# Transposing the row maxima of two sets at once, and loading them in four transfers a half

## The reference, cut to what matters

```python
scores = jnp.einsum('bhqd,bhkd->bhqk', q, k) / jnp.sqrt(jnp.asarray(HEAD_DIM, q.dtype))
weights = jax.nn.softmax(scores, axis=-1)
ctx = jnp.einsum('bhqk,bhkd->bhqd', weights, v)
```

## Time and profile before

| | us |
|---|---|
| median of three runs (575.12 to 579.55) | 578.35 |
| the profiled execution | 579.48 |
| its span in the trace | 577.7 |

### The profile page before, as it was taken

One profiled execution on the slowest core, in us unless ns is written; L12 is line 12 of the kernel. 1 busy time (PEld: TensorE's weight loads), 2 busy tenths in 40 slices (PEclk: granted clock), 3 DMA queues, 4 the chain that ended last, 5 costly groups with the idle time before them and its releaser, 6 DMA issues.

```text
span 577.7 us, 12491 instructions
## 1 busy us (share of the span) xinstructions
PE 486.3 (84%) x3970; PEld 404.6 (70%) x3970; DVE 349.5 (60%) x1226; ACT 315.4 (55%) x675; POOL 201.9 (35%) x429
## 2 busy tenths in 40 slices
PE   1447999899998899975799999999999897599980
PEld 1336777668776588964677877777777687599970
DVE  7886687688775146756587778678678433112203
ACT  2214776677766535553476666575566654245640
POOL 7140002221222222444211112442543657765650
PEclk9998999899999999995799999999999998789995
DMA  6314333242321992004454324234320110222107
GB/s 179 94 37 131 118 101 98 78 129 89 97 66 67 412 364 74 2 1 125 133 184 141 96 63 140 87 101 125 107 72 17 52 46 18 80 83 72 43 19 218
DMA packets 52267, 60.06 MB, mean 104 GB/s; under 512 B 7633, under 2 KB 43354, under 8 KB 50928
## 3 DMA queue, kind: packets, MB, share of 16 engines
q1 hardware_dynamic: 47248, 52.99, 29.3%
q0 software_dynamic: 2272, 4.24, 2.3%
q10 hardware_dynamic: 2688, 2.10, 1.1%
HBM read 30.01 MB, written 29.23 MB: 103 GB/s over the span
## 4 chain that ended last, share of the span: by engine, by line
PE 49%; issue 4%; DVE 4%; ACT 4%; DMA 4%; POOL 3%; SPq 1%; POOLq 0%; ACTq 0%; DVEq 0%
PE ps L1483 6%; PE ps L1536 5%; PE ps L1724 5%; PE ps L1714 5%; PE ps L1519 5%; PE ps L1539 5%; PE ps L1448 2%; PE ps L1450 2%; PE ps L1449 2%; ACT probs L901 2%; PE ps L1677 1%; PE ps L1548 1%; DMA k_blocks<-y_dram 1%; PE ps L1775 1%; DMA k_dram<-qk_parts 1%
## 5 line engine op out<-in xcount | busy, mean ns | idle before, releaser
L901 ACT ACTIVATE probs<-ps 128x512 f32<-128x512 f32 x256 | 146.7, 598 | 81.0 <-PE ps L1539 77.3
L1519 PE MATMUL ps<-k_blocks,q_stacks 128*128 128x256 f32 x512 | 119.4, 317 | 15.9 <-DVE row_max L1135 8.4
L1143 DVE CUSTOM_DVE_ANT_0 ps<-ps,mask_q 128x256 f32<-128x256 f32 x256 | 102.7, 452 | 37.5 <-PE ps L1519 36.6
L1539 PE MATMUL ps<-q_stacks,k_blocks 128*128 128x256 f32 x512 | 106.4, 292 | 1.0 <-DMA q_stacks<-maxT 0.8
L1135 DVE TENSOR_REDUCE row_max<-ps 128x2 f32<-128x512 f32 x128 | 84.3, 687 | 34.5 <-PE ps L1519 33.3
L1539 PEld LDWEIGHTS ps<-q_stacks,k_blocks 128*128 128x128 f32 x512 | 87.5, 190 | 21.0 <-issue 10.5
L1519 PEld LDWEIGHTS ps<-k_blocks,q_stacks 128*128 128x128 f32 x512 | 81.3, 197 | 22.6 <-DVE row_max L1135 12.2
L1483 PE MATMUL ps<-probs,v_aug 128*32 128x256 f32 x1024 | 69.4, 389 | 5.5 <-ACT probs L901 4.5
L763 POOL TENSOR_SCALAR max_split<-row_max 128x16 fp32r<-128x16 f32 x32 | 6.5, 204 | 182.6 <-DVE row_max L1135 79.6
L1536 PE MATMUL ps<-mask_k,neg_mask_eye 128*128 128x512 f32 x128 | 54.3, 424 | 0.4 <-DMA q_stacks<-maxT 0.4
L708 POOL DMA_INDIRECT y_dram<-x_ring x39 | 41.0, 1051 | 25.6 <-ACT x_ring L1000 19.9
(11 more groups left out here) (211 smaller groups left out, 836.7 us busy)
## 6 DMA issues: line engine op xcount, KB each, us to landing
slots_dram<-x_ring SPq DMA_DIRECT2D x1, 10400.0 KB, 29.5
q_stacks<-q_dram SPq DMA_DIRECT2D x32, 256.0 KB
q_dram<-qk_parts SPq DMA_DIRECT2D x16, 384.0 KB, 3.7
k_dram<-qk_parts SPq DMA_DIRECT2D x16, 384.0 KB, 4.0
k_blocks<-k_dram SPq DMA_DIRECT2D x128, 48.0 KB
x_ring<-slots_dram SPq DMA_DIRECT2D x39, 65.0 KB, 2.0
ctx_in<-ctx SPq DMA_DIRECT2D x16, 128.0 KB, 2.2
mask_in<-mask_Bx1xSxS_ik SPq DMA_DIRECT2D x8, 256.0 KB, 3.0
```

The source lines that it names most:

```text
L901: eng.activation(probs[:, n // HPS % 2, n % HPS, :, :].rearrange("p k q -> p (k q)"), ps[:, head_bank(BANKS_T, n)[0], :], ACT.Exp).then_in ...
L1143: last = eng.tensor_tensor_reduce(out=scored, in0=scored, in1=mask_q[1 - r][:, i, :], scale=1.0, scalar=-3.0e38, op0=ALU.add, op1=ALU.max, ...
L1519: mm = eng.matmul(ps[:, bank, i * S:(i + 1) * S], q_stack[r][:, st, i * P:(i + 1) * P], k_blocks[r][:, st, j, :], start=True, stop=True)
L1539: mm = eng.matmul(ps[:, bank, k * S:(k + 1) * S], k_blocks[r][:, st, j, k * P:(k + 1) * P], q_stack[r][:, st, :], start=(l == 0), stop=(l ...
```

## The change

`max_split` is laid out with the two sets of a half beside each other, so a tile's 16 columns (2 sets x 2 parts x 4 heads) are transposed at once. There are two transposes a half instead of four, each 16x128 out. ScalarE's copy is 16x256 instead of 8x512. In `maxT` the sets now lie on different partitions, so the loads into `q_stacks` are made for each set and part: four transfers a half, of four rows of 256 elements, instead of two of four rows of 512. The counts that are awaited go from 2 to 4 transfers.

```diff
-        maxT = sb("maxT", [2 * HPS, 2, 2, S])
+        maxT = sb("maxT", [2 * 2 * HPS, 2, S])
...
             eng.wait_ge(a.mT_sb, b * 2 + half + 1)
-            for part in range(2):
-                eng.dma_start(q_stack[r][part:part + (HPS - 1) * HR + 1:HR, 2 * half:2 * half + 2, :].bitcast(F32),
-                              maxT[part * HPS:(part + 1) * HPS, half, :, :]).then_inc(a.m_in[half], DMA)
+            for st in range(2):
+                for part in range(2):
+                    rows = slice((st * 2 + part) * HPS, (st * 2 + part + 1) * HPS)
+                    eng.dma_start(q_stack[r][part:part + (HPS - 1) * HR + 1:HR, 2 * half + st, :].bitcast(F32),
+                                  maxT[rows, half, :]).then_inc(a.m_in[half], DMA)
...
                 if after(b, 0):
-                    eng.wait_ge(a.m_in[half], b * 2 * DMA)
+                    eng.wait_ge(a.m_in[half], b * 4 * DMA)
                 elif l == 1:
-                    eng.wait_ge(att[0].m_in[half], NB * 2 * DMA)
+                    eng.wait_ge(att[0].m_in[half], NB * 4 * DMA)
                 bank = (BANK_M, BANK_O[0])[half]
-                eng.activation(maxT[:, half, :, :].rearrange("p s q -> p (s q)"), ps[0:2 * HPS, bank, :],
-                               ACT.Copy).then_inc(a.mT_sb, 1)
+                eng.activation(maxT[:, half, :], ps[0:2 * 2 * HPS, bank, 0:S], ACT.Copy).then_inc(a.mT_sb, 1)
...
                 if n % 8 == 0:
-                    eng.wait_ge(a.m_in[n // 8], (b + 1) * 2 * DMA)
+                    eng.wait_ge(a.m_in[n // 8], (b + 1) * 4 * DMA)
...
                 eng.wait_ge(a.m_split, b * 2 + half + 1)
-                for st in range(2):
-                    for i in range(NT):
-                        mm = eng.transpose(ps[0:2 * HPS, bank, st * S + i * P:st * S + (i + 1) * P],
-                                           max_split[:, i, half, st, :, :].bitcast(F32).rearrange("p m j -> p (m j)"),
-                                           ident[:, :])
+                for i in range(NT):
+                    mm = eng.transpose(ps[0:2 * 2 * HPS, bank, i * P:(i + 1) * P],
+                                       max_split[:, i, half, :, :, :].bitcast(F32).rearrange("p s m j -> p (s m j)"),
+                                       ident[:, :])
                 mm.then_inc(a.mT_ps, 1)
```

## The result

The changed kernel takes 584.03 us (median of 5 runs, 582.40 to 585.62) where the kernel before takes 578.81 (median of 5, 575.12 to 579.55). The ratio on record is 1.0119, its 95% interval 1.0090 to 1.0149; the quotient of these two medians is 1.0090, at the interval's lower end. A second series on another occasion gave 1.0111 (1.0072 to 1.0150), with medians 6.3 us apart. So the change costs 5.2 us by the first pair of medians and 6.4 to 6.9 by the ratios. Its profiled execution took 584.33 us with a span of 582.5 us, against 579.48 and 577.7 before.

The account below looks back on a forecast made before the run. The maxima transfers' landing bounds the first stage, TensorE's work the second. First stage +4.0, second -1.6 and clock +2.4 us give +4.8 on 579.48, so 584.3 us profiled and 583 us median, range 577 to 588.

Parts of the forecast that it names:

- Two more issues, 1.1 us: On SyncE's queue, each half's two added maxima transfers were to take 1.1 us more to issue.
- Both bounds: Limits for the two added issues on SyncE: 0.6 us at the k loads' pitch, 2.4 us with a landing added.
- The landing opens every batch of the first stage, 1.3 us behind the last issue: First stage: TensorE starts each batch when the last maxima transfer lands, about 1.3 us after its issue ends.
- faster rival: First-stage openings: the landing does not release them, added issues are hidden, transposes save 5.8 us, total 572.5 us; chance 0.06.
- Five waits for `max_split` swallow 2.7 us: At five first-stage openings, TensorE's waits for GpSimd's split, 2.7 us in all, were to absorb part of the delay.
- Transposes, 0.18 us a group: On TensorE, two transposes fewer save 0.18 us per group: 9 groups in the first stage, 15 in the second.
- The copy, 385 ns: ScalarE's copy was to fall from 578 to 385 ns, with 0.1 us left on the path where it releases SyncE.
- Both stages without the clock, +2.4 us: Both attention stages before clock effects: first stage +4.0 us, second stage -1.6 us, together +2.4 us.
- The second stage keeps its room: Second stage: the landing's 1.38 us to spare ahead of TensorE's opening was to shrink to 0.3 us and hold.
- Two more stretches at the lower clock, +2.4 us: TensorE behind the openings of batch 1 and the second stage: longer waits lower the clock, 1.2 us each.
- rival with the lower clock at nearly every opening: Steady batches' waits of 1.1 to 1.5 us also lower TensorE's clock, five more stretches, near 589 us; chance 0.17.
- The base: Starting time for the sum: the profiled execution's 579.48 us, 1.1 us above the runs' median of 578.35.

Follow-up runs that it names:

- e8: Changed kernel with half 0's rows of 256 each moved in two transfers of 4x128, eight in half 0 and four in half 1; 629.0 us, 1.0886 of before.
- e7: Kernel before with the second of half 0's two maxima transfers issued by ScalarE instead of SyncE; 576.7 us, 0.9996 of before.
- e10: The change in half 0 alone, half 1 as in the kernel before; 584.5 us, 1.0120 of before.
- e4: Changed kernel with only the first set's two transfers per half, the second set's maxima not loaded or subtracted; 574.7 us, 0.9960 of before.
- e1: Kernel before with four maxima transfers of 4x256 in both halves, old transposes and copy; 584.2 us, 1.0118 of before.
- e2: Kernel before with four maxima transfers in half 0 alone, two in half 1, old transposes; 585.2 us, 1.0128 of before.
- e6: Changed kernel with the second set's two transfers of half 0 issued by ScalarE, the first set's by SyncE; 578.0 us, 1.0008 of before.
- e3: Kernel before with four maxima transfers in half 1 alone, two in half 0, old transposes; 577.2 us, 1.0007 of before.
- e9: The change in half 1 alone, half 0 as in the kernel before; 574.0 us, 0.9939 of before.
- e11: Changed kernel with matmuls that nobody reads put ahead of TensorE's waits; 578.9 us, 1.0031 of before.

## Why the prediction was right, and where it was not

583 us was predicted, in a range of 577 to 588, and 584.0 came. The change costs 5.2 us by the first series' medians and 6.4 to 6.9 by the ratios, and the sum said 4.8. The mechanism was right: SyncE's two added issues delay the landing that opens the batches. That the number came so close is in part luck, since errors of several terms cancel. Its steps:

- **Two more issues, 1.1 us.** Right: 2.15 to 2.19 us for four. Both bounds are excluded (e8: 0.54 us each at eight).
- **The landing opens every batch of the first stage, 1.3 us behind the last issue.** Right for the kernel before (the table above). What the step missed is that a smaller transfer lands sooner: 1.15 to 1.26 us for 4x256, and 1.07 to 1.18 for the 4x128 of e8. The openings came later by 1.08 - 0.15 = 0.93 us and not by 1.1, some 1.3 us less over eight. The faster rival falls with the same table; at the opening that e7 lets one compare, the landing was last by 0.16 us.
- **Five waits for `max_split` swallow 2.7 us.** Right: 2.7 us before, none after.
- **Transposes, 0.18 us a group.** The size was 0.22. The count was wrong in the second stage: 15 groups were counted, and the 7 of half 0 give nothing. There the next matmul of the scores starts 0.35 us behind four transposes (376.40 to 376.75) and 0.34 behind two (382.74 to 383.08); ahead of its weight load the changed kernel's row names VectorE's `row_max`. The period fell by 0.23 where 0.36 was predicted; e10 shows the zero of half 0 by itself. For the first stage the step had this distinction and was right.
- **The copy, 385 ns.** 361 ns. The 0.1 us that it was to give SyncE at an opening did not come at the steady ones: the gap between the k loads and the group is 0.12 us before and 0.13 after (162.76 + 1.68 to 164.57).
- **Both stages without the clock, +2.4 us.** Span x clock rose by 1.8 to 2.0. Within it e4 and the changed kernel put the two issues at +5.0 to 5.4 us (e1 and e2 against before: +4.0 and +4.8); e4 against before, and the changed kernel against e1, put transposes and copy at -2.2 to -3.6. Each is a quarter to a half smaller than in the sum (7.2 and 4.8), with some 2 us of uncertainty in each difference, and the errors cancel. That is luck. The steady period was to be 18.4 and is 18.22.
- **The second stage keeps its room.** Right, and with more than the 0.3 us predicted. SyncE's group and TensorE's opening in a steady batch (answers to the earlier trace rows):

```profile
383.84 2.15 SPq L489 DMA_DIRECT2D q_stacks<-maxT  x4
```

```profile
387.50 0.49 PE L1520 MATMUL ps<-k_blocks,q_stacks 128*128 128x256 f32 x2
387.83 0.40 PE L1537 MATMUL ps<-mask_k,neg_mask_eye 128*128 128x512 f32 x1
```

  With the 1.18 us of the first stage the group would open TensorE at 385.99 + 1.18 = 387.17, and TensorE comes at 387.83, 0.66 us later, without a wait. e8 confirms it from the other side: 2.16 us more in the group, and waits of 1.26 to 1.69.
- **Two more stretches at the lower clock, +2.4 us.** This is the term that was mis-sized most: it is +4 to 5 us in the mean of the runs, with some 2 us of uncertainty. It named batch 1 and the second stage's opening. The second came (0.77 and 0.86 above, and likewise in both profiles of the changed kernel and those of e1, e2 and e10). It is not the maxima's wait alone that brings it: e6 has it behind the opening too (0.59) without such a wait, and e4 has a stretch of 0.57 just ahead of its opening (293 to 297 us) and 1.00 behind it. e3, e7 and e9 run at 1.00 there. Behind batch 1 the clock was 1.00 in the changed kernel's first profile and 0.66 in its second, which had a low stretch behind batch 2 as well and none behind batch 3. The step reasoned from which single wait had been followed by a low clock in one execution; between executions of one kernel it is not the same wait. The rival with the lower clock at nearly every opening did not come at waits of 0.7 to 1.4 us; it came at 2.8 to 3.3 us (e8), behind most openings.
- **The base.** The profiled execution of the kernel before had a clock of 0.951 and 28.3 us in the clock's share, where its 63 later runs have 24.0 to 25.3 in the mean. The two profiles at the head therefore show the same clock, 0.951, and hide the clock's part of the loss. That base was 1 to 2 us too high and the increment 2 us too small, which is why the predicted time came out closer than the working deserved.

The Trainium skill ("TensorE: Matmul & The Clock Gate", section on oscillation in real kernels) describes a kernel whose clock falls in every tile because the waits for transfers are long against the work between them, and says to arrange the work so that TensorE stays busy. e8 and e11 agree, at 0.921 and 0.9575 of mean granted clock against 0.950 of the changed kernel. The rule of "DMA: Bandwidth & Descriptors" (Rules for kernel authors), to join small transfers, agrees for half 0 (+7 us) and has no effect in half 1 (e3, 1.0007), where the queue is free. The fixed cost of 2.0 us that the prediction took from this page of the Trainium skill stands there for transfers that GpSimd issues. Here SyncE issues them, and the last issue of the maxima ends 1.07 to 1.44 us ahead of the openings that wait for it.

Still open: why the stores of q and k at batch 3 land early in some executions and late in others (below); why the changed kernel is no faster than e1 and e10, whose rows have more work; and why low stretches also stand in e4 and e6.

## What to carry to other kernels

In this kernel an added transfer cost its issue time only in the queue position that releases the next step, so make such a change where the queue has slack and keep the old form where it has none: here half 1 gave 3.5 us and half 0 cost 7. A missing bracket does not show that nothing was waited for: compare the distance from the releaser with openings where the wait is named. Before relieving a chain, look for the next one: here the exponentials ended 0.16 us ahead of the landing, and a landing 0.5 us earlier gave nothing that the runs can tell. Judge the clock by the mean granted clock over all runs, not by two profiles; in the changed kernel waits of about one microsecond went with 4 to 5 us of clock and 2 us of everything else.

## What the runs showed that I had not expected

- Useless matmuls in its waits made the changed kernel 5 us faster (584 to 579), with the period as it was.
- Half the bytes are issued in the same time but land 0.15 us sooner (1.33 to 1.18 us at a steady opening, and likewise at each of seven).
- An issue is not cheaper on another engine's queue: on ScalarE 0.53 us, as on SyncE, and there it delayed the exponential that TensorE opens behind by 0.25 us (two issues: 0.58).
- The time from the store of q at batch 3 to that batch's maxima group is 7.5 us in some executions (e1: 99.47 to 106.99; e3: 96.46 to 103.94) and 8.6 to 9.1 in others (before: 96.75 to 105.34; e6: 96.74 to 105.85), with no relation to the kernel: the changed kernel's two profiles have 8.9 (99.12 to 108.02) and 7.5 us (102.62 to 110.11). This alone moves the end of the first stage by over 1 us between single profiles. At the second stage's opening it was 5.7 to 8.7 us from the store of k to the load of q (before 286.76 to 292.49; e4 284.88 to 293.56).
